# Splitting the edge-list loads by shape over two DMA queues, and holding the first weight loads until x has landed, in a two-layer graph network

## What is computed

```python
def rgcn_conv(x, edge_index, edge_type, W_rel, W_root, bias):      # layer 0: 2 types, 1024 -> 286
    src, dst = edge_index
    out = x @ W_root + bias
    for r in range(NUM_REL):
        w = (edge_type == r).astype(x.dtype)
        msg = x[src] @ W_rel[r] * w[:, None]
        sums = segment_sum(msg, dst, num_segments=N)
        cnt = segment_sum(w, dst, num_segments=N)
        out = out + sums / jnp.maximum(cnt, 1.0)[:, None]
    return out
# layer 0: hidden + elu(rgcn_conv(rms_norm(hidden))) @ wo
# layer 1: u = rgcn of the same form with 8 types, 1024 -> 1024
#          z = concat([u, x]) @ w_gate + b_gate ;  h = tanh(u) * z + x * (1 - z)
x = _layernorm(x + layer0(x));  x = _layernorm(x + layer1(x))
```

## Time and profile before

| | |
|---|---|
| time, median of 3 runs | 891.17 us (891.15 to 892.2) |
| profiled execution | 891.17 us, of which its span is 889.2 us |
| PE busy | 834.6 us (94%) |
| DVE busy | 674.5 us (76%) |
| ACT busy | 447.7 us (50%) |
| POOL busy | 16.1 us (2%) |
| DMA | 30734 packets, 63.42 MB, mean 71 GB/s |

### The profile page before, as it was taken

How to read it: one execution, slowest core, us unless ns; L and a number is a source line. 1 busy time by engine, 2 the same in 40 slices (tenths; PEclk the granted TensorE clock), 3 DMA queues, 4 the chain that set the end, 5 groups by cost and what they waited for, 6 DMA issues and landing times.

```text
span 889.2 us, 16319 instructions
## 1 busy us (share of the span) xinstructions
PE 834.6 (94%) x6332; PEld 591.8 (67%) x6332; DVE 674.5 (76%) x975; ACT 447.7 (50%) x633; POOL 16.1 (2%) x38
## 2 busy tenths in 40 slices
PE   2569999899989999999999999999999999999996
PEld 1435574445876876876866867867868768769442
DVE  5985569689987778778778777677777787777877
ACT  3984555556465544445355356255354444445721
POOL 1000000000000000000000000000000000000000
PEclk9669999999999999999999999999999999999998
DMA  8100026120222021021120220220220210311302
GB/s 266 62 23 31 0 99 235 72 95 1 95 96 95 2 96 68 28 95 33 61 94 1 93 94 0 94 94 0 94 94 0 94 66 30 119 34 63 119 24 92
DMA packets 30734, 63.42 MB, mean 71 GB/s; under 512 B 1389, under 2 KB 5097, under 8 KB 30697
## 3 DMA queue, kind: packets, MB, share of 16 engines
q1 hardware_dynamic: 30181, 62.64, 19.9%
q10 hardware_dynamic: 516, 0.26, 0.1%
HBM read 57.71 MB, written 5.18 MB: 71 GB/s over the span
## 4 chain that ended last, share of the span: by engine, by line
PE 76%; DVE 16%; ACT 4%; issue 3%; DVEq 0%; POOL 0%; ACTq 0%; POOLq 0%
PE psP L1081 44%; PE psA L1151 19%; PE psP L928 5%; PE psA L917 3%; DVE wsplit L1326 2%; DVE wsplit L1320 2%; PE psP L1006 1%; DVE p_mem L1364 1%; PE psP L885 1%; DVE wsplit L1455 1%; PE psA L873 1%; DVE xT L1292 1%; DVE stats L1530 1%; DVE cu_mem L1574 1%; DVE p_mem L1363 1%
## 5 line engine op out<-in xcount | busy, mean ns | idle before, releaser
L1081 PE MATMUL psP<-wsplit,xT 128*128 128x256 f16 x2592 | 296.4, 273 | 3.2 <-ACT vec L767 2.8
L1081 PEld LDWEIGHTS psP<-wsplit,xT 128*128 128x128 f16 x2592 | 254.3, 98 | 37.5 <-issue 3.1
L1151 PE MATMUL psA<-p_mem,cu_mem 128*128 128x512 f16 x800 | 175.3, 379 | 0.0
L1081 PE MATMUL psP<-wsplit,x 128*128 128x256 f16 x1296 | 150.3, 273 | 1.7 <-DVE key_mem L1640 1.5
L1151 PEld LDWEIGHTS psA<-p_mem,cu_mem 128*128 (+1 forms) x800 | 78.2, 98 | 91.0
L1081 PEld LDWEIGHTS psP<-wsplit,x 128*128 128x128 f16 x1296 | 126.7, 98 | 16.8 <-issue 2.2
L1326 DVE SCALAR_TENSOR_TENSOR wsplit<-stage,sc,wsplit 128x1024 f16<-128x1024 f32 x90 | 114.8, 1279 | 27.2 <-ACT wsplit L611 27.2
L611 ACT ACTIVATE wsplit<-stage,sc 128x1024 f16<-128x1024 f32 x90 | 100.6, 1137 | 15.0 <-DVE sc L1228 9.1
L1605 DVE SCALAR_TENSOR_TENSOR cu_mem<-psA,coef,cu_mem 128x512 f32<-128x512 f32 x80 | 60.0, 750 | 32.9 <-PE psA L1151 30.9
L611 ACT ACTIVATE wsplit<-x,sc 128x1024 f16<-128x1024 f32 x54 | 61.7, 1143 | 39.2 <-PE psP L1081 32.5
L1326 DVE SCALAR_TENSOR_TENSOR wsplit<-x,sc,wsplit 128x1024 f16<-128x1024 f32 x54 | 69.2, 1282 | 10.3 <-ACT wsplit L611 10.2
(11 more groups left out here) (189 smaller groups left out, 800.8 us busy)
## 6 DMA issues: line engine op xcount, KB each, us to landing
stage<-in_L_gnn_weight SPq DMA_DIRECT2D x16, 2048.0 KB, 7.8
stage<-in_L_gnn_w_gate SPq DMA_DIRECT2D x4, 2048.0 KB, 7.8
x_home<-x SPq DMA_DIRECT2D x5, 512.0 KB, 2.6
x<-x_home SPq DMA_DIRECT2D x5, 512.0 KB, 5.6
stage<-in_L_gnn_W_rel SPq DMA_DIRECT2D x4, 572.0 KB, 11.1
x<-in_x SPq DMA_DIRECT2D x4, 512.0 KB, 9.6
xT<-in_L_gnn_root SPq DMA_DIRECT2D x1, 2048.0 KB, 8.0
stage<-in_L_gnn_root SPq DMA_DIRECT2D x1, 2048.0 KB, 7.8
```

The source lines that it names most:

```text
L1081: last = nc.tensor.matmul(psP[:, bank, (col + tt) * FB:(col + tt + 1) * FB], lhs[tt](a, c), split_block(n, b)[:, c, :], start=(first and t ...
L1151: last = nc.tensor.matmul(psA[:, (NT * h + t) % 2, :], cnt8[:, r, s, t * P:(t + 1) * P], p_part[h][a][:, s, :], start=(s == 0 and a == 0), ...
```

## The change

Three things are done.

1. **The edge DMAs are divided by shape, not by array.** SP issues the four main DMAs (DST, SRC, TYPE8, TYPE2, 125 rows of 640 bytes each). ACT issues the four tails (124 rows of 384 bytes each) after its wait for `edges_padded`. Before, each of the two issued two main DMAs and then two tails.
2. **One semaphore instead of two.** All eight count up `edges_loaded`, and DVE waits for 16 · 8 = 128 before `firsts`. The later wait for the types is gone.
3. **SP waits for all of x before it issues the first weight DMA.** Before, it issued them straight behind x.

```diff
-        nodes_loaded = sem("nodes_loaded")
-        types_loaded = sem("types_loaded")
+        edges_loaded = sem("edges_loaded")
...
-        def load_edges(engine, arrays, loaded):
-
-            for a, v in arrays:
-                engine.dma_start(edges[:, a, 0:RUN], v.rearrange("(p e) -> p e", e=RUN)).then_inc(loaded, 16)
-            engine.wait_ge(edges_padded, 2)
-            for a, v in arrays:
-                engine.dma_start(edges[0:EP - 1, a, RUN:SPAN],
-                                 v[RUN:EDGES].rearrange("(p e) -> p e", e=RUN)[:, 0:SPAN - RUN]).then_inc(loaded, 16)
-
         @block.sync
         def _(sp):
-            load_edges(sp, ((DST, dst_d), (SRC, src_d)), nodes_loaded)
-            for t in range(2):
-                sp.dma_start(x[:, t, :], x_d[t * P:(t + 1) * P, :]).then_inc(x_loaded[t], 16)
+            for a, v in enumerate((dst_d, src_d, t8_d, t2_d)):
+                sp.dma_start(edges[:, a, 0:RUN], v.rearrange("(p e) -> p e", e=RUN)).then_inc(edges_loaded, 16)
+            sp.dma_start(x[:, 0, :], x_d[0:P, :]).then_inc(x_loaded[0], 16)
+            sp.dma_start(x[:, 1, :], x_d[P:2 * P, :]).then_inc(x_loaded[1], 16)
...
             st0 = unit_weights(U_W0)[0]
+            for t in range(NT):
+                sp.wait_ge(x_loaded[t], 16 if t < NT - 1 else 32)
             for a in range(2):
...
         @block.scalar
         def _(act):
-            load_edges(act, ((TYPE8, t8_d), (TYPE2, t2_d)), types_loaded)
+            act.wait_ge(edges_padded, 2)
+            for a, v in enumerate((dst_d, src_d, t8_d, t2_d)):
+                act.dma_start(edges[0:EP - 1, a, RUN:SPAN],
+                              v[RUN:EDGES].rearrange("(p e) -> p e", e=RUN)[:, 0:SPAN - RUN]).then_inc(edges_loaded, 16)
...
-            dve.wait_ge(nodes_loaded, 64)
+            dve.wait_ge(edges_loaded, 16 * 8)
...
-            dve.wait_ge(types_loaded, 64)
```

## The result

| | before | with the change |
|---|---|---|
| median | 891.68 us (891.15 to 892.99, 4 runs) | 897.4 us (897.23 to 897.73, 4 runs) |
| span of the profiled execution | 889.2 us | 895.0 us |
| DVE starts `firsts` | 9.21 us | 15.95 us |
| first sorting matmul on PE | 12.90 us | 19.47 us |

The ratio is 1.0066, with a 95% interval of 1.0054 to 1.0079: **slower by 5.7 us**. The forecast was 898.1, the range 894.0 to 900.0. The record has 21 runs of the changed kernel in all, 897.08 to 898.77 us. (Lines of `kernel.py` have moved by 4 to 7, so L1255 of before is L1251 here, and L855 is L851.)

What follows compares the result with a forecast made beforehand. PE was 76% of the span, its start held by edge loads and POOL. Edges done on q1 at 8.5 us plus 7.6 for leftover tails put DVE at 16.1, not 9.21: 891.2 + 6.9 = 898.1 us, range 894.0 to 900.0.

Steps and rivals of the forecast that it cites:

- The mechanism and the sign: At the edge loads: tails on four engines alternate by packet with x, DVE starts 6.9 us later, kernel slower (0.88).
- the lag: On ACT's queue q10: packets by which it trails q1, 41 before, 60 with the later issue.
- the other bound that the prediction named: Beside the tails: all 156 x packets stand in the way at 20 per us; DVE at 17.0, +7.8 us.
- surplus: On q10: tails left when q1's main edge packets are done, 96 + 60 = 156, taking 7.6 us beside x.
- The hold: On SP's queue: weights wait for all of x, land at 37.2 us at the latest, 6.7 us of cover, no cost.
- the cap: On the tails' four engines: x has 156 packets there; any more tails would run at full pace behind it.
- Two rails of equal length: At the first sorting matmul: POOL to 12.87 us and edges to 12.76; a gain on edges alone is worth nothing.
- The shift: From the first sorting matmul to the end: the 6.9 us delay is kept, PE's clock adding 1 us either way.
- A: At the edge loads: several small packets go in one turn, tails don't get stuck, +0.9 us, 892.1; chance 0.10.
- B: On q10: fewer tails left, 40 to 80, +2 to +4 us, 893.2 to 895.2; chance 0.13.
- C: At ACT's L648: weights land after 43.9 us and become the wait, adding say 2 us, 900; chance 0.02.
- D: On PE: its clock meets the shifted work well while tails don't get stuck, faster, 889; chance 0.02.

Runs made afterwards that it cites:

- `x_behind_edges`: Changed kernel, with SP issuing x only when all eight edge DMAs have landed: 890.42 us, ratio 0.9994.
- `swapped_queues`: Changed kernel with the queues exchanged, ACT issuing the main edge DMAs and SP the tails ahead of x: 890.9 us, ratio 0.9997.
- `x_halves`: Changed kernel with each of the first four x tiles loaded as two DMAs of half rows, 2048 bytes a packet: 895.66 us, ratio 1.0057.
- `after_spread`: Changed kernel with each edge DMA cut in two, 112 rows and the rest: 891.5 us, ratio 1.0004.
- `after_again`: The changed kernel itself, run again as the base for two other kernels: 897.74 us, ratio 1.0083.
- `hold_only`: Kernel before, with SP's wait for all of x ahead of the first weight DMA as its only change: 891.15 us, ratio 1.0001.
- third set: Runs on one chip of the changed kernel again, without its wait ahead of the weights, with x in half rows, and nodes first; before: 890.14 us.
- `before_spread`: Kernel before, with each edge DMA cut in two, 112 rows and the rest: 887.66 us, ratio 0.9961.
- `wait_only`: Kernel before, with DVE's wait for the types moved up in front of `firsts`, DMAs unchanged: 894.38 us, ratio 1.004.

## Why the prediction was right, point by point

**The mechanism and the sign** were right. DVE's start was put at 16.1 us and was 15.95; the sorting at 19.8 and was 19.47. Turns by packet, four engines for the tails, x as what is in the way: `x_behind_edges`, `swapped_queues`, `x_halves` and `after_spread` each took one of these away, and the loss went or shrank as it should.

**The right start came from errors that cancel, and so in part by luck.** The prediction had 156 tails left when q1's mains are done, and put that time at 8.5 us. The last main left at 7.17 us, with 227 tails still to go, and at 8.5 us there were still 206 packets on q10. The term that was mis-sized is the lag. It allowed q10 0.55 us of later start and q1 50 packets per us meanwhile, and came to 60. In the trace q10's first packet left at 3.51 us instead of 2.05, so 1.46 us later, and q1 had sent 223 by then (0 to 3.5 us; there is no row of q10):

```profile
q1 hardware_dynamic: 223, 0.14, 16.6%
```

Four fifths of 223 are 178, and 96 + 178 = 274 would be left if the queues then took strict turns; it was 227. Strict turns thus say too much here, and how the other 47 got through is not shown. What kept the start at 16 us is, first, that x began to stand in the way earlier than forecast and, second, the other bound that the prediction named, x's 156 packets on these engines: x was nearly through at 14 us, and beyond it the tails run free, 77 in 1.5 us. So the sum gave the right start from a surplus that was too small, a time that was too late and a pace that was, at the end, too slow.

The surplus also differs between executions of the same kernel. `after_again` had 153 packets left on q10 at 8.5 us, passed them at 22.5 per us (8.5 to 14 us) beside x without being free of it, and started at 15.92. In that execution the forecast's 156 left at 8.5 us and 20.5 per us nearly fit.

**The hold** was rightly priced at nothing for the kernel before (`hold_only`) and wrongly for the kernel that was made: the prediction said "Nobody gains". Without the hold the changed kernel is 1.6 us slower. The likely reason is the empty q1 behind x, where the surplus is above the cap. It follows from the prediction's own remark that tails beyond the 156 run at full pace, which holds only if nothing comes after x.

**"Two rails of equal length"** was wrong. The prediction took the releaser that the profile names at L855 as what PE waited for. It was a late increment of a semaphore of which PE asks only the first. That PE's first matmuls need the constants of L503, as is said ahead of the prediction, is not so. POOL's rail ended at 10.29 + 0.33 = 10.62, not at 12.87, and it also moves with the loads. A gain on the edges is worth 3 us (`before_spread`), not nothing. For this change it made no difference, since the edges only got later.

**The shift** was kept to within a microsecond, and PE's clock took the rest, as allowed for. In the profiled executions it was 6.6 us at the sorting matmuls (19.47 against 12.90) and 7.2 at L545 (25.74 against 18.57), because 22 matmuls took 4.75 us instead of 4.16; at the end of the span it was 5.8. The piece that gave most back is a block of 60 matmuls at 254 us before, and at 261 us after:

```profile
253.88 8.38 PE L1081 MATMUL psP<-wsplit,xT 128*128 128x256 f16 x60 [2.82 <-ACT vec L767]
```

```profile
261.18 6.71 PE L1077 MATMUL psP<-wsplit,xT 128*128 128x256 f16 x60 [2.83 <-ACT vec L763]
```

The same work after the same pause took 1.67 us less. The busy time by stretch shows the clock (the columns are the length, the busy time and count of PE, PEld, DVE, ACT and POOL, the granted clock, DMA share and GB/s; 0.50 is 1.2 GHz, 1.00 is 2.4 GHz), first before, then after:

```profile
255.00:258.00 3.00, 3.00 (x17) 2.12 (x15) 2.97 (x3) 1.70 (x2) 0.00 (x0) 0.50 1.03 395
```

```profile
262.00:265.00 3.00, 3.00 (x30) 2.69 (x29) 2.97 (x3) 1.70 (x2) 0.00 (x0) 1.00 1.05 400
```

Before, the clock was at its lower level for a part of this block; after, it stayed at the upper. In the third set the changed kernel came out 7.6 us above before. The forecast of 6.9 lies between the two. The timed runs have no trace, but the record gives the mean granted clock of most. In the third set the runs of before at 0.978 and 0.979 have a median of 889.96 us (5 runs) and those at 0.975 and 0.976 one of 891.17 (4 runs); those of the changed kernel 896.9 (2 runs at 0.979) and 898.32 (3 at 0.976). With the clock alike the change costs 6.9 and 7.15 us there. For the 5.7 this can't be done: of the four runs of before only the profiled one has its clock on record, 0.975, while the changed kernel's profiled one had 0.979. That part of the gap to 6.9 is the clock is therefore likely and not shown.

**The rivals.** A (many small packets to a turn) is refuted by `x_halves`. B (a smaller surplus) did not happen: it was bigger in the profiled execution, and about as forecast in `after_again`. C (the weights as the wait) did not happen: no engine waits for them. They were issued from 15.8 to 18.6 us and landed within 9.2 us, so by 27.8 and not by 37.2, and the cover is larger than the prediction had it. D did not happen.

## What to carry to other kernels

A DMA's place is more than its queue: count the packets that each engine gets from each queue, and see what stands beside the last of them. A small load that something waits for must not share engines with a bulk load on the other queue; put it ahead of the bulk on the same queue, or spread it by giving it a row count that divides by 16 (112 and a rest here). With the queues alone exchanged the changed kernel was level with before (890.9 us against 890.88), and so it was with the rows alone (891.5); below before came only kernels with the rows spread, 887.66 and 886.45. And before a releaser named by the profile is taken as a bound, look up how many increments the waiting engine asks for.

## What the runs showed that was not expected

- **POOL's first instruction behind its memset comes sooner when the edges are spread.** Its `ident` started at 8.4 to 8.6 us in the four kernels with edge DMAs of 112 rows, and at 10.0 to 11.1 in all others, after an idle time for which the profile names no releaser. What POOL waits for there was not found.
- **DVE's instructions are longer beside POOL's tables**: the six comparisons 2.55 us instead of 1.36 (`wait_only`, `after_spread`), and an x normalisation 1.17 us instead of 0.75 (`swapped_queues`, at 13.46 us). A start that is moved can meet them or miss them, which is 1.2 us here.
- **The second queue starts late.** In the changed kernel ACT issued its first tail at 1.31 us, and q10's first packet left at 3.51. In `after_spread` the issue was at 1.30 and the first packet left at 2.33. In the meantime q1 sends more than it does beside a busy q10, 151 and 153 packets in the first 3 us (`after`, `after_again`). With the edges of before the two queues together sent 85, 114 and 135 (`before`, `wait_only`, `hold_only`). Why the first tail waits was not found.
